# Two-layer transformer block on one core: expert layer by indirect transfers to expert slots and back, in place of all experts on all tokens

## The chip, the cores and the metric

The kernel runs on one core of a Trainium2 chip. The core has five engines that work through their own instruction streams and meet only at semaphores: TensorE (PE; its weight loads are shown apart as PEld), VectorE (DVE), ScalarE (ACT), GpSimd (POOL) and SyncE (SP), which here only starts transfers. All engines but SP compute; TensorE writes into eight banks of PSUM, each 128 partitions by 512 floats. The metric is the device time of one execution in microseconds (us), and lower is better.

## What is computed

Four sequences of 1024 tokens with 128 features go through two layers. The second and third lines below are what the change is about: a router gives each token one of 8 experts, and each expert takes at most 512 tokens (positions are counted in token order, and the comparison is `pos < C`, with positions from 1); a token beyond that gets nothing from the expert layer.

```python
x = x + attention(layernorm(x))              # 16 heads, ALiBi, causal, (4, 1024, 128)
x = x + expert_layer(layernorm(x))           # 8 experts, 4096 tokens, C = 512
x = x + batch_attention(layernorm(x))        # for each position 0..1023: a 4x4 mixing of the sequences
x = x + dense(layernorm(x))                  # one 128x128 product

# expert_layer, x is (4096, 128)
probs = softmax(x @ Wr + br)
gate, idx = max(probs), argmax(probs)
mask = one_hot(idx, E)
pos = cumsum(mask, axis=0) * mask            # place of the token in its expert
mask = mask * (pos < C)
expert_in = gate * mask * x                  # sent to (expert, place)
h = relu(expert_in @ W1[e] + b1[e])
out = gate * mask * (h @ W2[e] + b2[e])      # taken back from (expert, place)
```

The batch attention mixes only the four sequences at one position, so a TensorE tile that holds all four sequences of 32 positions can do it with a mask (`samet`).

## The kernel before, in words

The program has two blocks, with a meeting of all engines between them. The first block is attention. A planner (`plan()`) writes out one order of scores, maxima, exponentials and weighted sums for TensorE, and the other engines follow it. SP's stream in that block carries the operands, the rows of maxima (`q_operand<-max_rows_sb`), the weighted sums to and from DRAM and, late, the residual rows `x_res`. The change touches there the residual loads (`load_residuals`), the bias added to them on GpSimd (`add_bias`) and the transfers placed in SP's stream.

The second block is `later_stages`. Its work comes in 8 chunks of 4 tiles of 128 tokens. Every tile holds 32 positions of all four sequences, so that one layout serves from the attention's output to the last store.

- First stage: for each chunk the sums are divided (`divide`, `reciprocals`), projected (`project`), added to the residual (`add`) and normalised. GpSimd raises to the power -0.5 in three groups, SPANS; ScalarE and VectorE share `apply`. Transposes (`turned`) and logits follow.
- Routing: once for all 32 tiles, on VectorE with three TensorE products for the counts (L1094 to L1128), down to one `gate` for each token, which is 0 for a dropped one.
- Expert loop: 64 slots, one for each pair of chunk and expert. In a slot TensorE multiplies all 512 tokens of a chunk by one expert's W1 (`expert_in`, L1273), adds a large negative number in the columns of tokens of other experts (L1274, `big` by `noth`), ScalarE applies relu with the bias (L1390), and TensorE adds the product with W2 into one bank (`expert_out`, L1282). After 8 experts the bias b2 comes by L1286 and `moe_out` adds the result times the gate. So each token goes through all 8 experts, and 7 of them give zero.
- Batch attention and the dense layer: their steps (t3, u, s, mask, mix, t4, f) are placed by the table SLOTS between the expert slots of the next chunk. Within one chunk they are a chain over four engines; only the steps of the last chunk have no expert slots beside them.

## Time and profile before

| what | us |
|---|---|
| median of 3 runs (798.9 to 801.77) | 799.12 |
| the profiled execution, whole | 797.04 |
| its span from the first to the last instruction | 795.3 |
| TensorE busy in the span | 662.6 |
| VectorE busy | 515.1 |
| ScalarE busy | 448.7 |
| GpSimd busy | 153.8 |
| mean granted clock of TensorE | 0.921 of full |

The profile gives, for each stretch or group of instructions, the time in which an engine was busy, and what ended an idle time before an instruction. TensorE's clock has two levels, 1.2 and 2.4 GHz; a granted clock of 0.50 is the lower and 1.00 the upper. A duration is quoted with the clock where that matters: four transposes take longer at 0.50 than at 1.00. Names such as `ring`, `bank` and `sums` are the PSUM tensors.

### The profile page before, as it was taken

To read this page: it belongs to the slowest core of one execution; us is meant where nothing else is said; L and a number is where in the kernel's file an instruction comes from. 1 tells how busy PE (TensorE), PEld (TensorE's weight loads), DVE (VectorE), ACT (ScalarE), POOL (GpSimd) and SP (SyncE) were. 2 spreads that over 40 slices of the span, in tenths; PEclk is the share of its full clock that TensorE was granted. 3 is DMA by queue.
4 is the path that set the end of the run, shared out by engine and by line. 5 is a ranking of instruction groups with operands and counts; after the bars stand their busy time and mean duration, and the time that the engine had idled before them with its cause. 6 is when DMAs were issued, how large, how long until landed. Compare 5 with 4: busy or idle time off the path is not lost.

```text
span 795.3 us, 14721 instructions
## 1 busy us (share of the span) xinstructions
PE 662.6 (83%) x5478; PEld 315.9 (40%) x5478; DVE 515.1 (65%) x1024; ACT 448.7 (56%) x765; POOL 153.8 (19%) x245
## 2 busy tenths in 40 slices
PE   3656988999989899889899885765799999999953
PEld 2431333333323233333333220455356666666643
DVE  5999788998888888889788830574221345333443
ACT  2950777788777887778777884032234443344310
POOL 2660122212221222212451221030000011010110
PEclk9995899999999999999999998685699999999965
DMA  6494645422212341332203000100000000000001
GB/s 157 133 200 122 160 109 139 107 46 49 52 34 48 72 76 36 75 72 50 50 7 77 6 10 10 28 1 0 1 0 1 10 6 14 14 14 6 9 13 27
DMA packets 49806, 40.58 MB, mean 51 GB/s; under 512 B 9772, under 2 KB 44724, under 8 KB 49724
## 3 DMA queue, kind: packets, MB, share of 16 engines
q1 hardware_dynamic: 43576, 37.22, 20.2%
q10 hardware_dynamic: 6160, 2.43, 1.3%
q8 instruction: 44, 0.72, 0.4%
q14 instruction: 26, 0.21, 0.1%
HBM read 22.32 MB, written 17.04 MB: 49 GB/s over the span
## 4 chain that ended last, share of the span: by engine, by line
PE 62%; DVE 19%; ACT 6%; issue 6%; POOL 3%; DMA 2%; SPq 0%; POOLq 0%; DVEq 0%; ACTq 0%
PE sums L756 15%; DVE neg_max L783 10%; PE ring L735 10%; PE ring L1282 9%; PE ring L1273 8%; PE bank L707 5%; ACT probs L804 5%; PE ring L1274 3%; PE bank L701 2%; DVE probs L506 2%; PE ring L1286 1%; PE bank L1319 1%; PE bank L1222 1%; PE bank L1330 1%; PE ring L718 1%
## 5 line engine op out<-in xcount | busy, mean ns | idle before, releaser
L783 DVE TENSOR_REDUCE neg_max<-bank 128x2 f32<-128x1024 f32 (+2 forms) x320 | 342.8, 1115 | 60.9 <-PE bank L707 58.8
L804 ACT ACTIVATE probs<-ring 128x512 f32<-128x512 f32 (+4 forms) x481 | 301.8, 681 | 79.8 <-PE ring L735 66.8
L735 PE MATMUL ring<-q_operand,k_operand 56*128 56x512 bf16 (+3 forms) x768 | 164.3, 333 | 18.2 <-ACT probs L804 14.5
L756 PE MATMUL sums<-probs,v_all 128*9 128x512 f32 (+3 forms) x1536 | 162.4, 495 | 2.7 <-POOL probs L837 2.1
L707 PE MATMUL bank<-k_operand,q_operand 54*128 54x512 bf16 (+3 forms) x768 | 144.5, 338 | 7.0 <-DVE v_all L514 5.3
L837 POOL TENSOR_SCALAR_AFFINE_SELECT probs<-probs 128x512 f32<-128x512 f32 x128 | 80.2, 635 | 215.6 <-ACT probs L804 214.7
L735 PEld LDWEIGHTS ring<-q_operand,k_operand 56*128 56x128 bf16 x768 | 50.2, 94 | 152.6 <-ACT probs L804 110.5
L1390 ACT ACTIVATE hid<-ring,b1c 128x512 f32<-128x512 f32 x64 | 44.0, 687 | 81.9 <-PE ring L1274 81.7
L701 PE MATMUL bank<-masks 64*128 64x128 bf16 (+2 forms) x768 | 71.9, 224 | 5.2 <-DVE neg_max L783 4.9
L1282 PE MATMUL ring<-w,hid 128*128 128x128 f32 x512 | 74.9, 290 | 0.0
L1273 PE MATMUL ring<-xgt,w 128*128 128x512 f32 x128 | 69.0, 621 | 1.2 <-ACT noth L1382 1.2
L1282 PEld LDWEIGHTS ring<-w,hid 128*128 128x128 f32 x512 | 62.8, 193 | 14.5 <-issue 12.9
L991 POOL TENSOR_TENSOR rs<-ve,half_pow 128x4 f32<-128x4 f32 x16 | 16.1, 1007 | 233.1 <-DVE ve L1011 233.1
L707 PEld LDWEIGHTS bank<-k_operand,q_operand 54*128 54x128 bf16 x768 | 46.1, 97 | 24.5 <-DVE neg_max L783 14.8
L701 PEld LDWEIGHTS bank<-masks 64*128 64x128 bf16 x768 | 36.7, 95 | 37.9 <-DVE neg_max L783 25.4
L1143 DVE SCALAR_TENSOR_TENSOR x_res<-ring,gate,x_res 128x128 f32<-128x128 f32 x32 | 9.0, 344 | 58.8 <-PE ring L1286 58.8
L756 PEld LDWEIGHTS sums<-probs,v_all 128*9 128x9 f32 x1536 | 23.2, 88 | 53.5 <-issue 39.8
L1179 DVE TENSOR_TENSOR res<-x_res,bank 128x512 f32<-128x512 f32 x8 | 5.5, 688 | 54.2 <-PE bank L1330 54.2
L718 PE MATMUL ring<-identb,max_parts 128*32 128x128 bf16 x32 | 7.1, 221 | 24.7 <-POOL max_parts L854 23.5
L1274 PEld LDWEIGHTS ring<-noth,big 8*128 8x128 bf16 x64 | 5.8, 91 | 50.0 <-issue 50.0
L1024 DVE RECIPROCAL denominators<-denominators 128x128 f32<-128x128 f32 x1 | 1.0, 952 | 37.3 <-DMA denominators<-weighted_sums 37.3
L1274 PE MATMUL ring<-noth,big 8*128 8x512 bf16 x64 | 25.1, 392 | 0.0
(156 smaller groups left out, 654.8 us busy)
## 6 DMA issues: line engine op xcount, KB each, us to landing
q_operand<-q_rows SPq DMA_DIRECT2D x64, 96.0 KB, 3.4
k_operand<-k_rows SPq DMA_DIRECT2D x32, 192.0 KB, 4.0
q_rows<-qk_parts SPq DMA_DIRECT2D x36, 128.0 KB, 2.4
k_rows<-qk_parts SPq DMA_DIRECT2D x36, 128.0 KB, 2.4
weighted_sums<-osum SPq DMA_DIRECT2D x128, 18.0 KB
sums_in<-in_L_attn_x SPq DMA_DIRECT2D x4, 512.0 KB, 7.3
q_operand<-max_rows_sb SPq DMA_DIRECT2D x128, 2.0 KB
sums_in<-weighted_sums SPq DMA_DIRECT2D x4, 512.0 KB
```

The lines of the kernel that those rows point to most:

```text
L701: nc.tensor.matmul(ends, masks[rows, 0, a, :], masks[rows, 1, a:a + 1, 64 * a:P].to_broadcast([64, len(pairs), P - 64 * a]), start=a == 0, ...
L707: last = nc.tensor.matmul(ps[:, h, w * j:w * j + w], q_op[rows, buf, t // CH, p, P * (t % CH):P * (t % CH) + P], k_op[rows, buf, p, CW * k ...
L735: last = nc.tensor.matmul(psS[:, bank, w * j:w * j + w], k_op[rows, buf, p, P * kb:P * kb + P], q_op[rows, buf, c, p, q0:q0 + w], start=Tr ...
L756: last = nc.tensor.matmul(psO[32 * i:32 * i + HD + 1, q0:q0 + w], v_all[:, n, kb, i, :], probs[:, u % NPROBS, i // 2, i % 2, 0:w], start=u ...
L783: nc.vector.tensor_reduce(neg_max[:, n % 2, slot, kc, :, pairs[0]:pairs[-1] + 1, t % CH], src, AX.X, ALU.max, negate=True).then_inc(a_read, 1)
L804: nc.scalar.activation(dst, src, ACT.Exp).then_inc(ring_read, 1)
L837: nc.gpsimd.affine_select(out=tri, in_=tri, compare_op=ALU.is_ge, fill=0.0, base=0, pattern=[[0, GH], [1, P]], channel_multiplier=-1).then ...
L991: nc.gpsimd.tensor_tensor(rs[:, :], ve[:, :], half_pow[:, 0:CH], ALU.pow).then_inc(pw_ready, 1)
L1273: nc.tensor.matmul(psZ[n % 2], w1[:, e, :], xgt[:, j % 2, :], start=True, stop=False)
L1274: nc.tensor.matmul(psZ[n % 2], big[:, e, :], noth[:, j % 2, :], start=False, stop=True).then_inc(z_psum, 1)
L1282: nc.tensor.matmul(psY[:, P * i:P * i + P], hid[:, n % 3, P * i:P * i + P], w2[:, e, :], start=(e == 0 and i == 0), stop=False, skip_group ...
L1390: nc.scalar.activation(hid[:, n % 3, :], psZ[n % 2], ACT.Relu, bias=b1c[:, e:e + 1]).then_inc(hid_ready, 1)
```

## The change

It does the expert layer by moving tokens. (1) The residual is held in token order in `rows`, 258 numbers a token: the gated normalised row (XG), the row before the expert layer (X1), the token's number (TOK) and its gate. (2) The first stage of `later_stages` runs in sequence order, tick by tick, with power, scales and `apply` for each chunk, all `apply` on ScalarE. (3) Places are computed in three rounds (tiles 0-15, 16-23, 24-31), by products with a triangle and with ones; place and expert give a row number, `slot`. (4) GpSimd starts 32 indirect transfers, one for each tile, that write each token's 1032 bytes to its row of `expert_rows` in DRAM; dropped tokens have a row number out of bounds. `expert_rows` is cleared by 16 transfers placed in SP's stream during attention. (5) SP waits for all 32, loads each expert's 512 rows, and the experts run once each, on their own rows. (6) GpSimd starts 32 indirect transfers that write each finished row (512 bytes) to its token's row of `x2_rows`; SP waits for all of them. (7) SP loads `x2_rows` in the old layout (32 positions of four sequences), and batch attention and the dense layer run as a loop of 9 ticks, with mask on GpSimd and the scaling of both norms on ScalarE.

The three loops at the end of the diff are VectorE's first stage, TensorE's experts and TensorE's last loop.

```diff
+            def clear_slots(sp, i):
+                n = 2 * P
+                sp.dma_start(slots_dram[n * i:n * i + n, :].rearrange("(p a) f -> p (a f)", a=2),
+                             fill[:, :, :].rearrange("p a f -> p (a f)").bitcast(F32)).then_inc(slots_clear, 16)
...
+                    elif kind == "A" and n >= 5 and args[0] % 8 == 4 and clears:
+                        clear_slots(sp, clears.popleft())
...
-        for j in range(CHUNKS):
-            sp.wait_ge(res_ready, j + 1)
...
+        for k in range(CHUNKS):
+            sp.wait_ge(x1_ready, k + 1)
+            sp.dma_start(x2_dram[CW * k:CW * k + CW, :].rearrange("(u p) d -> p u d", p=P),
+                         rows[:, CH * k:CH * k + CH, X1:X1 + D]).then_inc(x1_out, 16)
+        sp.wait_ge(scattered, 16 * TILES)
+        sp.wait_ge(x1_out, 16 * CHUNKS)
+        for e in range(E):
+            sp.dma_start(es[:, e, :, :].rearrange("p a f -> p (a f)"),
+                         slots_dram[CAP * e:CAP * e + CAP, :].rearrange("(p a) f -> p (a f)", a=CH)).then_inc(es_in[e], 16)
+        sp.wait_ge(x2_out, 16 * E * CH)
+        for j in range(CHUNKS):
+            for b in range(B):
+                src = x2_dram[S * b:S * b + S, :].rearrange("(u t) d -> t u d", t=32)
+                sp.dma_start(x2[32 * b:32 * b + 32, CH * j:CH * j + CH, :], src[:, CH * j:CH * j + CH, :]).then_inc(x2_in[j], 16)
...
+        def send_rows(u):
+            pool.wait_ge(row_ready, u + 1)
+            nc.gpsimd.indirect_dma_start(
+                out=slots_dram, out_offset=bass.IndirectOffsetOnAxis(ap=slot[:, u:u + 1], axis=0), in_=rows[:, u, :],
+                in_offset=None, bounds_check=E * CAP - 1, oob_is_err=False).then_inc(scattered, 16)
+        def send_tokens(e, a):
+            pool.wait_ge(ye_ready, e + 1)
+            nc.gpsimd.indirect_dma_start(
+                out=x2_dram, out_offset=bass.IndirectOffsetOnAxis(ap=es[:, e, a, TOK:TOK + 1].bitcast(U32), axis=0),
+                in_=ye[:, e, a, :], in_offset=None, bounds_check=B * S - 1, oob_is_err=False).then_inc(x2_out, 16)
...
+        for t in range(TICKS):
+            if t < CHUNKS:
+                add(t)
+                if t + 1 < CHUNKS:
+                    divide(t + 1)
+                scales(t)
...
+        for e in range(E + 1):
+            if e + 1 < E:
+                columns_of(e + 1)
+            if e < E:
+                expert_in(e)
+            if e >= 1:
+                expert_out(e - 1)
...
+        for t in range(CHUNKS + 1):
+            if t >= 1:
+                mixed(t - 1)
+            if t < CHUNKS:
+                t3(t)
+                u_of(t)
+            if t >= 1:
+                t4(t - 1)
+            if t < CHUNKS:
+                scores(t)
+            if t >= 1:
+                f(t - 1)
```

On GpSimd, in the second block, stand before only the powers of the norms.

```order
L988 TENSOR_TENSOR rs<-ve,half_pow 128x16
L988 TENSOR_TENSOR rs<-ve,half_pow 128x8 x2
L991 TENSOR_TENSOR rs<-ve,half_pow 128x4 x16
L261 UNCONDITIONAL_BRANCH
```

And now, at the same place of GpSimd's stream:

```order
L998 TENSOR_TENSOR rs<-ve,half_pow 128x4 x8
L1002 DMA expert_rows<-rows,slot 4096x258 x32
L1008 DMA x_rows<-ye,rows 4096x128 x32
L1014 TENSOR_TENSOR rs<-ve,half_pow 128x4
L1018 TENSOR_TENSOR ee<-ee,samet 128x512
L1014 TENSOR_TENSOR rs<-ve,half_pow 128x4 x2
L1018 TENSOR_TENSOR ee<-ee,samet 128x512
```

All 64 indirect transfers stand in one row between the powers of the first stage and those of the last, and the mask `ee<-ee,samet` has come from VectorE to GpSimd.

On TensorE, late in the second block of the kernel before, the steps of batch attention stand singly between expert products (a step of one chunk: L1305 is u, L1309 the scores, L1325 the transposes t4).

```order
L1305 MATMUL bank_0<-xt,aqk 128x512
L1273 MATMUL ring<-xgt,w 128x512
L1274 MATMUL ring<-noth,big 128x512
L1282 MATMUL ring<-w,hid 128x128 x4
L1309 MATMUL bank_0<-ut,xt 128x128 x4
L1325 MATMUL bank_1<-ident,xn 128x128 x4
L1273 MATMUL ring<-xgt,w 128x512
L1274 MATMUL ring<-noth,big 128x512
L1282 MATMUL ring<-w,hid 128x128 x4
L1330 MATMUL bank_1<-wft,xt 128x128 x4
```

And now, one tick of the last loop on TensorE, from one t3 (L1326) to the next:

```order
L1326 MATMUL bank_0<-ident,xe 128x128 x4
L1333 MATMUL bank_0<-xt,aqk 128x512
L1357 MATMUL ring<-ident,xn 128x128 x4
L1340 MATMUL bank_1<-ut,xt 128x128 x4
L1365 MATMUL ring<-wft,xt 128x128 x4
L1349 MATMUL bank_1<-xe,ee 128x129 x2
L1349 MATMUL ring<-xe,ee 128x129 x2
L1326 MATMUL bank_0<-ident,xe 128x128 x4
```

No product stands between the steps that is not itself a step of the chunk or of the chunk before; t4 of the chunk before stands ahead of the scores of this one.

On SP, after attention, stood only the stores; now three more kinds of transfer stand ahead of them.

```order
L972 DMA x_rows<-rows 128x4x128 x8
L977 DMA rows<-expert_rows 128x1032 x8
L983 DMA xn<-x_rows 32x4x128 x32
L988 DMA out<-res 32x4x128 x32
```

The expert loads stand behind a wait for all 32 transfers to the slots, the loads of `x2_rows` behind one for all 32 transfers back.

## Rows read from the trace of the kernel before

**Rows 1.** Busy time by stretches of the second block (us, instruction counts, granted clock, DMA)

```profile
502.60:548.65 46.05, 36.63 (x176) 29.67 (x176) 26.90 (x113) 10.96 (x24) 6.40 (x3) 0.72 0.00 1
548.65:560.60 11.95, 0.82 (x3) 0.28 (x3) 10.92 (x37) 0.42 (x1) 0.00 (x0) 0.50 0.00 0
560.60:759.20 198.60, 196.56 (x1050) 123.00 (x1050) 68.56 (x312) 75.46 (x122) 13.09 (x13) 0.97 0.03 8
759.20:795.30 36.10, 15.31 (x55) 11.63 (x54) 15.50 (x68) 3.46 (x6) 3.02 (x3) 0.54 0.08 20
```

**Rows 2.** In order of time: batch attention of the last chunk, no expert work beside it

```profile
765.38 2.09 PE L1319 MATMUL bank<-xe,ee 128*128 128x129 f32 x8 [6.17 <-DVE ee L1157]
767.26 1.06 PE L1301 MATMUL bank<-ident,xe 128*128 128x128 f32 x4
767.77 1.13 DVE L1168 SCALAR_TENSOR_TENSOR x_res<-bank,inv,x_res 128x128 f32<-128x128 f32 x4
768.35 0.59 ACT L1401 COPY xt<-bank 128x512 f32<-128x512 f32 x1 [12.36 <-PE bank L1301]
768.99 2.08 PE L1305 MATMUL bank<-xt,aqk 128*128 128x512 f32 x2 [0.68 <-ACT xt L1401]
774.48 0.63 ACT L1412 ACTIVATE ee<-th 128x512 f32<-128x512 f32 x1
775.64 2.07 PE L1330 MATMUL bank<-wft,xt 128*128 128x128 f32 x8 [0.97 <-ACT xt L1417]
...
790.93 0.69 DVE L1179 TENSOR_TENSOR res<-x_res,bank 128x512 f32<-128x512 f32 x1 [3.96 <-PE bank L1330]
```

**Rows 3.** Busy time by short stretches, the granted clock (columns as in rows 1)

```profile
525.00:530.00 5.00, 5.00 (x20) 3.97 (x19) 3.19 (x17) 2.69 (x6) 1.64 (x1) 0.50 0.00 0
530.00:535.00 5.00, 2.83 (x25) 2.73 (x24) 4.01 (x23) 2.16 (x6) 0.81 (x1) 0.99 0.02 5
...
770.00:775.00 5.00, 4.00 (x14) 2.53 (x12) 1.99 (x12) 1.70 (x3) 1.01 (x1) 0.50 0.00 0
```

**Rows 4.** In order of time (start, duration): where the second block begins

```profile
502.63 0.95 DVE L1024 RECIPROCAL denominators<-denominators 128x128 f32<-128x128 f32 x1 [37.29 <-DMA denominators<-weighted_sums]
...
509.17 0.69 DVE L1039 TENSOR_TENSOR x_res<-x_res,ring 128x512 f32<-128x512 f32 x1 [1.02 <-PE ring L1203]
```

**Rows 5.** In order of time: pieces of a norm, and a scaling on ScalarE

```profile
522.32 1.65 ACT L1353 ACTIVATE xn<-x_res,nt,rs 128x128 f32<-128x128 f32 x4 [29.58 <-DVE nt L1060]
...
760.40 0.87 DVE L1006 BATCH_NORM_STATS2 stats<-x_res 128x6 f32<-128x128 f32 x4
761.31 0.38 DVE L1009 BATCH_NORM_AGGREGATE mv<-stats 128x2 f32<-128x6 f32 x4
761.73 0.17 DVE L1011 TENSOR_SCALAR ve<-mv 128x4 f32<-128x4 f32 x1
761.98 1.01 POOL L991 TENSOR_TENSOR rs<-ve,half_pow 128x4 f32<-128x4 f32 x1 [13.28 <-DVE ve L1011]
```

**Rows 6.** GpSimd by shape: busy us, mean ns of one, idle before

```profile
L862 POOL TENSOR_TENSOR x_res<-x_res,bob 128x512 f32<-128x512 f32 x8 | 10.2, 1271 | 0.0
...
L988 POOL TENSOR_TENSOR rs<-ve,half_pow 128x16 f32<-128x16 f32 x1 | 2.9, 2914 | 27.2 <-DVE ve L1051 27.2
```

**Rows 7.** SP's issues of one transfer to DRAM (duration ns: min/median/max)

```profile
L671 SPq DMA_DIRECT2D weighted_sums<-osum x8: 264/315/317, 485.0 to 493.8; - x8
```

**Rows 8.** Transfers by line: count, KB each, us from issue to landing

```profile
x_res<-in_L_attn_x SPq DMA_DIRECT2D x4, 512.0 KB, 5.3
out<-res SPq DMA_DIRECT2D x32, 64.0 KB, 1.8
```

**Rows 9.** GB/s moved, in 40 equal slices of the span

```profile
GB/s 157 133 200 122 160 109 139 107 46 49 52 34 48 72 76 36 75 72 50 50 7 77 6 10 10 28 1 0 1 0 1 10 6 14 14 14 6 9 13 27
```

**Rows 10.** In order of time: products of the same shapes at the upper clock

```profile
653.76 1.06 PE L1309 MATMUL bank<-ut,xt 128*128 128x128 f32 x8
654.66 0.60 PE L1325 MATMUL bank<-ident,xn 128*128 128x128 f32 x4
```

879 lines of the change are left out of this document (432 added, 447 removed).

## The prediction, made before the changed kernel was run

> **What bounds the kernel now.** I read first the busy time by stretches. After attention, which ends at 502.6 us, the second block has four stretches [rows 1]: 46.1 us to the logits, 12.0 of routing with TensorE all but idle, 198.6 in which TensorE is busy for 196.6 (expert products for all tokens, with the steps of batch attention and the dense layer between them), and 36.1 in which the last chunk's chain runs out. So TensorE's work bounds the long stretch, and most of that work is multiplied by zero. Next come the rows of the last chunk, where the chain over the engines lies open: each step starts 0.03 to 0.05 us after the one before it ends, and the products take twice as long as earlier, since the granted clock is 0.50 [rows 2, 3]. That open chain is what I need, because the new last loop consists of it.
>
> **First stage (new), until the first row can be sent.** It starts as before: the reciprocal ends the wait at 502.6, the first add begins at 509.2 [rows 4]. A tick on VectorE is the add 0.69, statistics 0.87 and 0.38, variance 0.17, GpSimd's power 1.01 (the division, 0.69, lies under it) and four short operations of 0.2: 3.9, with the passages between engines 4.2 [rows 2, 5]. TensorE's tick is two sets of eight pieces (up to 2.07 each), one of transposes (1.06) and the logits (at most 2.07, eight pieces with fewer columns): 7 at the lower clock, half at the upper [rows 2, 10]. The clock moved between both levels in this stage before [rows 3]; I take 5.0 a tick, between the ends 4.2 and 7. Seven ticks bring the eighth add to 544.2. Ahead of the first places TensorE still has the transposes and logits of two chunks (3.0), then 16 products with ones; an fp32 piece costs 0.26 (2.07 for eight) [rows 2], these are bf16 and mostly shorter, I take 0.13, 2.1 in all. Placing is eight short operations (2.0), gating one tile 0.4 on ScalarE (1.65 for four) [rows 5]. The first row can go at **551.5**. Two more rounds of some 10 us make the last rows ready near 571.
>
> **Sending, 32 indirect transfers.** They stand in one row on GpSimd, and everything later waits for all of them. No row shows an indirect transfer. Below, SP starts a small plain one in 0.32 [rows 7], but SP makes no list of 128 addresses. Above, GpSimd's dearest operation here is 2.91 [rows 6]. I take **1.3**, near GpSimd's pass over 128 x 512 elements, 1.27 [rows 6], as the kind of work that this engine does in software over 128 partitions; 0.32 and 2.91 stay for the range. 32 x 1.3 = 41.6 brings the last issue to 593.1; the rows, ready by 571, are not the bound. Landing takes 2.0 (1.8 for a store of 64 KB [rows 8]): 595.1.
>
> **Experts.** SP loads 528 KB an expert. The first lands 5.3 later, as 512 KB do [rows 8]; the next follow by 2.6 each if the fastest slice so far, 200 GB/s, holds [rows 9]. On TensorE the transposes of the third expert stand ahead of the first W2 product, so the first result waits for the third load, 10.6 after issue; then 1.06 + 2.08 + 2.07 on TensorE, 0.69 and 1.13 on VectorE [rows 2], 0.3 of passages: 17.9, so 613.0. From there GpSimd's other 32 issues bound: an expert costs TensorE 5.2 at the lower clock and 2.7 at the upper, four issues 5.2. 41.6 lead to 654.6, landing, four loads' issue and the landing of these (2.0 + 1.8 + 1.8 [rows 8]) to **660.2**. What the change removes is the whole of the 198.6: 64 expert slots become 8. What takes their place up to here is 102 us (551.5 to 653, of which 83 are issues).
>
> **The last loop.** Before, these steps cost only their TensorE time, since expert products filled the gaps. Now there is nothing to fill them, and a tick is a ring. From the end of one chunk's scores: tanh 0.6, exponential 0.63, the copy 0.59 for the dense product of the chunk before and that product 2.07 (it stands ahead of the mixing on TensorE; GpSimd's mask, 1.27 [rows 6], is ready sooner), mixing 2.09; on VectorE reciprocals 0.25, weighting 1.13, moments 1.59 and the scales of the next chunk 0.8, which stand behind them; ScalarE's scaling 1.65; transposes 1.06, copy 0.59, u 2.08, copy 0.59, ScalarE's second scaling 1.65, its transposes 1.06, the next scores 2.07 [rows 2, 5]. Sum 20.5, with 15 passages of 0.05 **21.2 us**. TensorE is busy for 10.4 of them. At 4.00 of 5 us busy in short pieces the clock stayed at 0.50 [rows 3], so I take the lower level. The first chunk's scores and exponential come 13.2 after the load (moments, power, scales, scaling, the same products), seven periods are 148.4, the way out from the last exponential 16.2: 660.2 + 177.8 = 838.0, and the last store adds 3.7, as now (790.93 + 0.69 to 795.3 [rows 1, 2]).
>
> **Attention.** SP gets 16 more transfers of 264 KB, each in front of rows of maxima for which TensorE waits later. At 200 GB/s one holds up the next by 1.3, so the bounds are 0 and 21; a gain is excluded, as nothing is taken from this stream. The rows of maxima have slack and the transfers are spread over eight groups of heads; I take 0.
>
> **Sum.** 841.7 for the span against 795.3. The profiled execution took 797.04, 1.7 more than its span, and the median of the runs is 2.1 above that: 843.4 and **845.5**; I forecast 845.
>
> **Weighed against the Trainium skill.** The traces show a store of 64 KB landing after 1.8 [rows 8], while SP starts the next after 0.32 [rows 7], so transfers overlap. The Trainium skill (DMA: Bandwidth & Descriptors, Anatomy of one DMA) gives about 2.0 us fixed for a transfer from GpSimd plus its bytes at 436 GB/s. Were 64 of them to run one after another, that would be an estimated 142 in place of 83, and the time 905; no row here shows whether they overlap.
>
> **Rivals.** (a) Issues as cheap as SP's, 0.32. Then the rows' readiness bounds the sending (571 in place of 593, -22) and TensorE and the loads bound the experts (seven periods of about 3, -19): 804. For it: transfers overlap on SP. Against: GpSimd takes 1.01 even for 128 x 4 powers [rows 5]. (b) The faster side: TensorE's clock rises in the last loop and stays. Then four products of a tick lose 1.01 each and two sets of transposes 0.46 [rows 2, 10], the period is 16.2, and the loop with its ends is 40 shorter: 805; the kernel is faster than 799 if besides an issue costs less than 1.2, and with 1.0 it takes 786. For it: dense product and mixing follow one another without a gap for 4.2 us, and 5.0 busy of 5 were followed by 0.99 [rows 3]. Against: 5.6 us of idling follow each time. (c) Transfers of GpSimd do not overlap; each holds the next until it lands. By the 1.8 of a store [rows 8] that is 64 x 1.8 = 115 for 83: 877. (d) An issue costs what GpSimd's dearest operation does, 2.91: 64 x 1.6 more, 948.
>
> **Chances.** Forecast with issues of 1.0 to 1.75: 0.64 (826 to 874 by 64 x the price). (a) 0.09, (b) 0.10, (c) 0.10, (d) 0.07. The range leaves out (b) and (d): **800 to 885**, with the cost in attention and the first stage's clock (4.2 to 7 a tick, -6 to +14) in it. Half a per cent is about what a measurement of this kernel can tell from no change. Faster by more: 0.10; within: 0.05 (a good part of (a), since 804 is near the bound); slower: 0.85.
>
> **What would show it.** In the changed kernel's trace: mean length of GpSimd's stretch with 32 issues (1.3 each; 0.3 and 2.9 are the rivals'); VectorE and TensorE idle through both of them; a period of 21 between the stores of the chunks, with granted clock 0.50 (16 and 1.00 for (b)); attention ending within 2 us of 502.6. It would be wrong if the price of an issue is off by 0.5 (32 us), if the chunk ring overlaps more than I see, or if the cleared rows hold up attention.

## The result: 3% slower, and where the time went

The changed kernel took 822.57 us in the median of four runs, 820.86 the fastest, beside 799.01 for the kernel before in the same comparison. The fourth run, 836.65, had a lower granted clock (0.733 in place of 0.81 to 0.82) and does not enter the ratio. The ratio is 1.031, with a 95% interval of 1.027 to 1.035. The forecast was 845 in a range of 800 to 885. The direction and the range held; the time came 22 us below the forecast. The profiled execution took 823.1, with a span of 821.1 against 795.3 before.

I read the busy time by stretches first, as for the kernel before. This is the view of the changed kernel, with the stretches cut at the events that the sum used; the columns are those of [rows 1]: the stretch, its length, busy time (and instructions) of PE, PEld, DVE, ACT and POOL, granted clock, DMA share, GB/s.

```profile
0.00:504.10 504.10, 416.42 (x4195) 152.18 (x4195) 393.76 (x497) 358.63 (x612) 130.83 (x227) 0.94 0.36 86
504.10:550.60 46.50, 32.17 (x218) 29.35 (x218) 32.14 (x146) 17.46 (x44) 8.07 (x8) 0.79 0.15 46
550.60:591.50 40.90, 8.20 (x80) 7.55 (x79) 9.06 (x48) 7.11 (x24) 31.40 (x32) 0.50 0.16 55
591.50:606.20 14.70, 9.80 (x43) 6.91 (x44) 2.32 (x6) 4.46 (x8) 0.01 (x1) 0.64 0.75 289
606.20:647.00 40.80, 11.02 (x70) 8.42 (x68) 12.19 (x35) 5.73 (x9) 31.33 (x32) 0.66 0.09 27
647.00:651.60 4.60, 0.00 (x0) 0.00 (x0) 0.00 (x0) 0.00 (x0) 0.03 (x1) 0.50 0.28 81
651.60:664.80 13.20, 5.26 (x14) 3.00 (x14) 3.64 (x24) 4.04 (x8) 1.05 (x1) 0.50 0.46 134
664.80:801.70 136.90, 64.89 (x230) 47.17 (x230) 41.12 (x234) 41.98 (x91) 22.69 (x21) 0.59 0.05 12
801.70:821.10 19.40, 6.99 (x28) 6.00 (x28) 4.80 (x22) 2.66 (x6) 2.28 (x2) 0.50 0.12 27
```

Rows 1 had 198.6 us in which TensorE was busy for 196.6. That stretch is gone. In its place stand two stretches of 41 us in which GpSimd issues without pause and the others mostly wait (third and fifth line), 15 us between them in which loads and the first experts run, and a last loop of 137 us in which TensorE is busy for 65. The change took away 45% of TensorE's busy time in the second block (138.3 us of products where there were 249.3, and most of what is left runs at the lower clock) and put more waiting than that in its place: from its first operation the block takes 317.4 us (503.7 to 821.1) where it took 292.7 (502.6 to 795.3).

**The sends.** The groups of the page for GpSimd (line, engine, operation, names, count, then busy us and mean ns, then idle time before):

```profile
L1008 POOL DMA_INDIRECT x_rows<-ye,rows x32 | 31.4, 980 | 24.2 <-DVE ye L1155 15.3
...
L1002 POOL DMA_INDIRECT expert_rows<-rows,slot x32 | 31.4, 982 | 13.7 <-issue 7.9
```

An indirect transfer of 128 rows keeps GpSimd for 0.98 us, whether its rows are long (`expert_rows`, the first stage) or short (`x_rows`). Between two of them lie 0.30 us in which the engine waits for nothing that is shown. The pitch is 1.28, and 32 of them are the 41 us.

**The last loop.** One tick of the changed kernel at the lower clock, in order of time (start, duration, engine, line, operation, names, and the idle time before with its releaser), some operations left out:

```profile
703.47 0.57 ACT L1475 COPY xt<-ring 128x512 f32<-128x512 f32 x1
703.64 1.27 POOL L1018 TENSOR_TENSOR ee<-ee,samet 128x512 f32<-128x512 f32 x1 [11.61 <-ACT ee L1470]
704.09 2.07 PE L1365 MATMUL ring<-wft,xt 128*128 128x128 f32 x8 [1.82 <-ACT xt L1475]
...
706.81 1.07 PE L1349 MATMUL ring<-xe,ee 128*128 128x129 f32 x4
707.92 0.17 DVE L1183 RECIPROCAL inv<-bank 128x2 f32<-128x2 f32 x1 [12.95 <-PE ring L1349]
...
708.19 0.61 DVE L1188 SCALAR_TENSOR_TENSOR xn<-bank,inv,xn 128x128 f32<-128x128 f32 x2
...
709.35 0.87 DVE L1163 BATCH_NORM_STATS2 stats<-xn 128x6 f32<-128x128 f32 x4
...
711.63 1.65 ACT L1446 ACTIVATE xe<-xn,nt 128x128 f32<-128x128 f32 x4 [7.59 <-DVE nt L1177]
...
713.33 1.12 PE L1326 MATMUL bank<-ident,xe 128*128 128x128 f32 x4 [5.45 <-ACT xe L1446]
...
715.12 2.07 PE L1333 MATMUL bank<-xt,aqk 128*128 128x512 f32 x2 [0.68 <-ACT xt L1456]
717.23 0.58 ACT L1458 COPY ut<-bank 128x512 f32<-128x512 f32 x1 [2.16 <-PE bank L1333]
717.71 1.65 ACT L1446 ACTIVATE xn<-xn,nt 128x128 f32<-128x128 f32 x4
719.41 1.12 PE L1357 MATMUL ring<-ident,xn 128*128 128x128 f32 x4 [2.22 <-ACT xn L1446]
...
720.32 1.91 PE L1340 MATMUL bank<-ut,xt 128*128 128x128 f32 x8
722.27 0.60 ACT L1465 ACTIVATE th<-bank 128x512 f32<-128x512 f32 x1 [2.91 <-PE bank L1340]
722.90 0.63 ACT L1470 ACTIVATE ee<-th 128x512 f32<-128x512 f32 x1
```

This is the open chain of [rows 2], but of every chunk: nearly always one engine at a time. Where the chain passes from one engine to another, the next step begins 0.03 to 0.06 us after the end of the one before. Between the mixing and the next chunk's transposes stands VectorE: it weights the mixed rows (L1188), takes their moments (from L1163 on), and only then makes the scales of the next chunk (L1174 to L1177), which need nothing of this one. VectorE waits 12.95 us for the mixing, GpSimd 11.61 for the exponential, once in every tick. The distances between the eight masks are 19.1, 19.7, 20.0, 20.0, 18.2, 20.0 and 20.0 us, 19.6 on average.

The granted clock of 0.59 says less than it seems to. This is the same tick in three parts (columns as above):

```profile
704.05:708.00 3.95, 3.79 (x16) 3.50 (x16) 0.08 (x1) 0.00 (x0) 1.83 (x2) 0.50 0.00 0
708.00:711.00 3.00, 0.00 (x0) 0.00 (x0) 2.84 (x17) 0.00 (x0) 0.01 (x1) 1.00 0.00 0
711.00:723.60 12.60, 6.01 (x18) 3.75 (x18) 3.25 (x18) 5.66 (x13) 1.00 (x1) 0.52 0.09 21
```

After the dense product and the mixing (3.79 us of TensorE) the upper level was granted, for 3 us in which TensorE had nothing to do, and it was gone again before the next product.

### The profile page after: what moved, and what is told of

Same layout as the page of the kernel before. It is cut to its first block, busy times and chain, and to the rows that moved or that the text cites. A ratio compares the mean times of both kernels' runs of the same rounds, so it can differ in the third digit from the quotient of the medians.

```text
span 821.1 us, 13686 instructions
## 1 busy us (share of the span) xinstructions
PE 554.7 (68%) x4875; PEld 260.6 (32%) x4875; DVE 499.0 (61%) x1010; ACT 442.1 (54%) x799; POOL 227.7 (28%) x323
## 4 chain that ended last, share of the span: by engine, by line
PE 46%; DVE 19%; ACT 12%; issue 9%; POOL 8%; DMA 3%; SPq 1%; POOLq 0%; DVEq 0%; ACTq 0%
PE sums L772 15%; PE ring L751 10%; DVE neg_max L799 9%; PE bank L723 5%; ACT probs L820 5%; POOL x_rows L1008 3%; POOL expert_rows L1002 2%; PE bank L1333 2%; PE bank L717 2%; PE bank L1340 2%; PE ring L1365 2%; ACT xn L1446 2%; DVE probs L517 1%; ACT xe L1446 1%; PE bank L1326 1%
## 5 line engine op out<-in xcount | busy, mean ns | idle before, releaser
L1446 ACT ACTIVATE xe<-xn,nt 128x128 f32<-128x128 f32 x32 | 13.2, 482 | 89.9 <-DVE nt L1177 89.9
L1326 PE MATMUL bank<-ident,xe 128*128 128x128 f32 x32 | 8.9, 435 | 77.8 <-ACT xe L1446 77.8
L1008 POOL DMA_INDIRECT x_rows<-ye,rows x32 | 31.4, 980 | 24.2 <-DVE ye L1155 15.3
L1018 POOL TENSOR_TENSOR ee<-ee,samet 128x512 f32<-128x512 f32 x8 | 10.2, 1270 | 91.8 <-ACT ee L1470 91.8
L1002 POOL DMA_INDIRECT expert_rows<-rows,slot x32 | 31.4, 982 | 13.7 <-issue 7.9
L1163 DVE BATCH_NORM_STATS2 stats<-xn 128x6 f32<-128x128 f32 x64 | 14.0, 281 | 34.7 <-DMA xn<-x_rows 31.7
L1386 ACT ACTIVATE xn<-rows,nt,rs 128x128 f32<-128x128 f32 x32 | 13.2, 482 | 38.9 <-DVE nt L1080 38.9
L1326 PEld LDWEIGHTS bank<-ident,xe 128*128 128x128 f32 x32 | 5.7, 217 | 79.8 <-ACT xe L1446 79.8
L1151 DVE TENSOR_TENSOR yb<-ring,b2b 128x512 f32<-128x512 f32 x8 | 5.5, 690 | 38.6 <-PE ring L1307 38.6
L1293 PE MATMUL bank<-ident,rows 128*128 128x128 f32 x32 | 6.3, 332 | 33.4 <-DMA rows<-expert_rows 33.3
```

Of the source, the lines that this page charges most:

```text
L1002: nc.gpsimd.indirect_dma_start(out=slots_dram, out_offset=bass.IndirectOffsetOnAxis(ap=slot[:, u:u + 1], axis=0), in_=rows[:, u, :], in_of ...
L1008: nc.gpsimd.indirect_dma_start(out=x2_dram, out_offset=bass.IndirectOffsetOnAxis(ap=es[:, e, a, TOK:TOK + 1].bitcast(U32), axis=0), in_=ye ...
L1326: last = nc.tensor.transpose(psT3[:, P * i:P * i + P], xe[:, j % 2, i, 0:D], ident[:, :])
L1446: last = nc.scalar.activation(dst, x2[:, CH * j + i, :], ACT.Identity, bias=nt[:, z, 1, i:i + 1], scale=nt[:, z, 0, i:i + 1])
```

## The experiments

Twelve runs were made in three groups of four. The kernels of one group ran on the same chip beside the kernel before (median 797.0, 798.7 and 794.3 us in the three). Times are medians, ratios are to the kernel before of the same group. `after_again` is the changed kernel itself and `f_late_b` is `f_late` once more; all others but `best`, `best2` and `best2_fill` differ from the changed kernel in one thing (`early` in two that go together). Eight of the twelve, the first and the third group, hold stalls of up to some 12 us that are the subject of part C, so their whole times are not to be set beside those of the second group.

### A. The last loop: clock, order, overlap

**filled**: does the granted clock set a quarter of a tick?

```diff
+        def busy(n):
+            for i in range(n):
+                nc.tensor.matmul(banks[7][:, 0:P], ident[:, :], aqk[:, :], start=True, stop=True)
         for t in range(CHUNKS + 1):
             if t >= 1:
                 mixed(t - 1)
+                busy(10)
             if t < CHUNKS:
                 t3(t)
+                busy(1)
                 u_of(t)
+                busy(4)
...
                 scores(t)
+                busy(3)
```

> The changed kernel with 18 products of 128x128 on constants into an unused bank put into TensorE's idle stretches of every tick of the last loop (10 ahead of the mixing, 1 ahead of u, 4 behind it, 3 behind the scores); nothing reads them. At the lower clock they take about 0.52 us each and fit the gaps of 5.4, 0.7, 2.2 and 1.8 us that the trace of the changed kernel shows. Theory A, the granted clock sets a quarter of each tick: the chain of one tick holds 9.9 us of products at the lower clock, which are 5.3 at the upper one, so if the fillers bring the clock up, the seven periods fall from 19.6 to about 15.5 us, the way out by 2, and the time from 822.6 to about 790 (ratio to the kernel before 0.99). Theory B, the products are not what a tick waits for (it is the other engines' chain): with the clock up the periods stay near 19 and the time near 820. If the clock stays at 0.50 the run shows only that fillers cost nothing: 822 to 826.

The ten stand behind the mixing, ahead of the next transposes, and not ahead of the mixing as the expectation says. It took 813.87 us, ratio 1.020 (1.014 to 1.025), with some 11 us of the stalls of part C. Two ticks of it by stretches (columns as above):

```profile
711.08:727.58 16.50, 10.81 (x70) 8.95 (x70) 6.16 (x35) 6.06 (x14) 3.25 (x3) 0.90 0.07 17
760.14:777.15 17.01, 11.88 (x70) 9.87 (x70) 6.17 (x35) 6.06 (x14) 3.24 (x4) 0.80 0.07 15
```

The clock is 0.8 to 0.9 in place of 0.59, and a tick takes 16.7 us on average where the changed kernel has 19.6. That is 2.9 less, not the 4.1 of theory A and far from theory B's 0.6. Most of the missing part is in one product. u stands behind the transposes and ScalarE's copy, and it still runs at the lower clock, for the whole or a part, in each of the seven ticks, as here:

```profile
713.42 2.40 PE L1370 MATMUL sums<-aqk,ident 128*128 128x128 f32 x20
...
720.36 2.08 PE L1333 MATMUL bank<-xt,aqk 128*128 128x512 f32 x2 [0.39 <-ACT xt L1464]
...
725.15 1.06 PE L1340 MATMUL bank<-ut,xt 128*128 128x128 f32 x8
```

The fillers (x20 are ten products) end near 715.8, TensorE stands idle until 719.0, and u, a little later, takes 2.08; the scores, which stand behind four fillers and the second transposes, take 1.06. So the mechanism of rival (b) is real: the clock costs about 3 us a tick of the average 19.6, and 3.5 of a tick that is all at the lower level. But the kernel as it is doesn't get it back, and fillers that leave one gap don't get all of it.

**f_late**: the dense product of a chunk behind the next mixing instead of ahead of it.

```diff
             if t >= 1:
                 mixed(t - 1)
+            if t >= 2:
+                f(t - 2)
...
                 scores(t)
-            if t >= 1:
-                f(t - 1)
+        f(CHUNKS - 1)
```

> The changed kernel with one order changed: on TensorE the dense product f of a chunk stands behind the next chunk's mixing instead of ahead of it. Theory A, a tick is one chain through TensorE's queue and f (2.07 us from the copy's end) stands in it ahead of the mixing by 1.2 us (the mask ended 704.91, the mixing began about 706.1): each of seven periods loses 1.2 us, 822.6 becomes about 814 (ratio to the kernel before 1.02). Theory B, another chain of the same length runs through f, its addition and the buffers that they free: no change, 822. The last chunk's f is where it was, so the way out doesn't change.

It took 827.85 us, ratio 1.038 (1.033 to 1.043): 5 us more than the changed kernel in its own comparison. The loop itself did get shorter, as its masks show:

```profile
675.15 1.27 POOL L1018 TENSOR_TENSOR ee<-ee,samet 128x512 f32<-128x512 f32 x1 [10.51 <-ACT ee L1471]
...
807.23 1.26 POOL L1018 TENSOR_TENSOR ee<-ee,samet 128x512 f32<-128x512 f32 x1 [11.61 <-ACT ee L1471]
```

The seven periods are 132.1 us against 136.9: theory A, though smaller. In the six profiles with the unchanged loop they are 133.7 to 137.3, by how many ticks had the upper level for the mixing, so the gain is to be read from ticks of one kind. A tick at the lower clock is 19.13 in place of 19.97 (0.84, where I had written 1.2), and the ticks in which the mixing falls into the upper clock are 18.2 in both kernels: there f takes 1.16, and the mixing begins 0.18 after the mask's end with it and 0.05 without. The 5 us are lost elsewhere: the first mask comes at 675.15 and not at 664.82. That is the subject of part C.

**pipelined**: the next chunk made independent of this one's mixing.

```diff
+        for t in range(2):                     # VectorE
+            moments_in(t)
+            normal_scales(0, t)
         for t in range(CHUNKS + 2):
+            if t >= 2:
+                add_out(t - 2)
+            if t < CHUNKS:
+                mix(t)
+                if t + 2 < CHUNKS:
+                    moments_in(t + 2)
+                normal_scales(1, t)
+                if t + 2 < CHUNKS:
+                    normal_scales(0, t + 2)
...
+            mask(t)                            # GpSimd
+            power_of(1, t)
+            if t + 2 < CHUNKS:
+                power_of(0, t + 2)
...
+                mixed(t)                       # TensorE
+                t3(t + 1)
+                u_of(t + 1)
+                scores(t + 1)
+                f(t - 1)
+                t4(t)
```

ScalarE follows in the same order: scaling of t+1, copy of t-1, copies of t+1, second scaling of t, tanh and exponential of t+1.

> The changed kernel with the last loop alone rewritten: the same instructions, but moments, power and scales of chunk t+2 are made in tick t, so that the normalization, scores and exponentials of chunk t+1 need nothing of chunk t's mixing, and f and its copy are one tick later. Theory A, the 19.6 us of a tick come from the order, in which VectorE makes the next chunk's scales only behind the mixing's sums: with the two chains side by side a tick falls to what the longer chain and TensorE's 9.3 us of products at the lower clock allow, about 12 us; seven periods save 53 us and the time is about 769 (ratio to the kernel before 0.96). If the denser TensorE also gets the upper clock, about 755. Theory B, the time of a tick is bound by buffers that two chunks share and by queues (ScalarE's 6 us, VectorE's 6 us): 16 us a tick, about 797.

It took 771.47 us, ratio 0.966 (0.961 to 0.971), with 11.4 us from mask to mask on average. Theory A held (about 12 a tick and 769 were expected), although some 12 us of stalls (part C) are in this time, so that 769 was met in part by luck. The same instructions in another order make the seven periods 57 us shorter, 79.5 in place of 136.9, so the 19.6 were no engine's bound. The clock is not what did it: in best, which has the same loop, ticks with a granted clock of 0.50 to 0.53 take 11.5 us as well.

### B. The sends

**half_sends**: are the issues the path?

```diff
         for e in range(E):
-            for a in range(CH):
+            for a in range(CH // 2):
                 send_tokens(e, a)
...
-        sp.wait_ge(x2_out, 16 * E * CH)
+        sp.wait_ge(x2_out, 16 * E * CH // 2)
```

> The changed kernel with 16 of the 32 transfers that send the experts' results back (two of four for each expert); half of the results are left out, so the time is only a price. Theory A, the stage is one queue of issues on GpSimd at 1.28 us each and all of it lies on the path: 16 x 1.28 = 20.5 us less, 802 us, the level of the kernel before. Theory B, the experts' work or the landings set the end of the stage: 5 us less or nothing, 817 to 822.

It leaves out half of the results, so its time is only a price. It took 810.1 us, ratio 1.019 (1.012 to 1.026). In the same group f_late_b, which has all 32, took 829.2. From the first to the last of these issues there are now 21.9 us (611.83 to 633.72), where f_late_b has 45.6 (611.00 to 656.63). 16 issues at 1.28 are 20.5, and 19 are seen in the whole time, although f_late_b's loop is the faster by some 5. What is left of the 23.7 between 21.9 and 45.6 goes with the stalls of part C, of which half_sends has fewer in this stage. Theory B's 5 us are excluded: the issues lie on the path.

**half_rows**: is the price one of rows?

```diff
-                ...ap=es[:, e, a, TOK:TOK + 1].bitcast(U32), axis=0),
-                in_=ye[:, e, a, :],
+                ...ap=es[0:64, e, a, TOK:TOK + 1].bitcast(U32), axis=0),
+                in_=ye[0:64, e, a, :],
```

> The changed kernel with each of the 32 transfers that send the experts' results back cut from 128 rows to 64; half of the results are left out, so the time is only a price. Theory A, GpSimd's 0.97 us for one such transfer is work for each row: it falls to about 0.6 us and the second stage of sends takes 29 us instead of 41, 12 us less in all. Theory B, it is a fixed price of one instruction: 0.97 us stays, the stage takes 40.8 us and the time stays within 1 us of the changed kernel on this chip.

It too leaves out half of the results. It took 818.75 us, ratio 1.026 (1.022 to 1.031), 4 us below the unedited kernel of its group (822.8); its five runs lie between 815.2 and 823.3, and the stage of these sends is 2.1 us shorter (37.8 from first to last issue in place of 39.9). The group of these issues, from the lines of half_rows:

```profile
L1008 POOL DMA_INDIRECT x_rows<-ye,rows x32 | 29.2, 913 | 23.8 <-DVE ye L1155 15.2 <-issue 8.5
```

Half of the rows take 0.91 us in place of 0.98. Nearly all of the price belongs to the instruction (theory B), and about 0.001 us, an estimate from this difference, to a row. Fewer transfers would help; smaller ones don't.

**early**: begin the sends a round sooner.

```diff
-    ROUNDS = [(0, 16), (16, 24), (24, 32)]
-    ROUND_AT = [CHUNKS - 2, CHUNKS, CHUNKS + 2]
+    ROUNDS = [(0, 8), (8, 16), (16, 24), (24, 32)]
+    ROUND_AT = [CHUNKS - 4, CHUNKS - 2, CHUNKS, CHUNKS + 2]
...
         for k in range(CHUNKS):
             power(k)
+            if k == CHUNKS - 2:
...
+                for u in range(3):
+                    send_rows(u)
```

> The changed kernel with four rounds of choosing (8 tokens' tiles each) in place of three (16, 8, 8), so that the first 8 tiles have their slots a round earlier, and three of the 32 sends issued between the last two of the first stage's powers on GpSimd. Theory A, the sends are one queue of 32 x 1.28 us which begins when the first round is placed: it begins 10 to 11 us earlier, less about 3 us that one more round costs VectorE; 7 to 9 us less than the changed kernel on the same chip. Theory B, the end of the sends is set by the last round (its tiles are placed last) or by the stores behind: no gain, up to 3 us lost by the added round.

It took 814.04 us, ratio 1.020 (1.015 to 1.026), 8.8 less than the unedited kernel of the group. The first send is at 544.0 in place of 553.3, the first mask at 660.5 in place of 666.7. Of the gain 6.2 us stand before that mask; the loop, which is the same, happened to be 1.8 shorter in this profile. Theory A: a queue that bounds is worth starting early, even at the price of one more round on VectorE.

**clears_late**: the 16 clears behind attention instead of in it.

```diff
-                    elif kind == "A" and n >= 5 and args[0] % 8 == 4 and clears:
-                        clear_slots(sp, clears.popleft())
...
                 load_sums(sp, B - 1)
+                while clears:
+                    clear_slots(sp, clears.popleft())
```

> The changed kernel with the 16 clears of the slots issued behind attention, ahead of the first stage's stores, instead of inside attention. Theory A, the clears cost attention the 1.1 us by which it ends later than in the kernel before (503.69 against 502.63): it ends near 502.6, and since the sends begin 46 us later the clears' 16 issues at 0.32 us are hidden: 821.5 (within 0.3% of the changed kernel). Theory B, the 1.1 us is spread of the executions: attention ends anywhere between 502 and 504.5, the time is the same. Theory C, the clears now collide with the first stage's stores and loads and the sends wait for them: up to 10 us longer, 832.

It took 836.8 us, ratio 1.047 (1.042 to 1.053), the worst of all. Theory C, but at another place than it said. SyncE's queue and VectorE's first operation of the second block, in order of time:

```profile
500.57 0.59 SPq L328 DMA_DIRECT2D denominators<-weighted_sums  x1
501.21 10.80 SPq L440 DMA_DIRECT2D expert_rows<-fill  x16
...
512.46 0.95 DVE L1049 RECIPROCAL denominators<-denominators 128x128 f32<-128x128 f32 x1 [43.39 <-PEq L371]
```

In f_late, of the same group, the reciprocal starts at 502.64 and the first addition at 509.13. Here they start at 512.46 and 517.94. SyncE needs 10.80 us for the 16 issues, 0.68 each where a single one takes 0.32 [rows 7]. Meanwhile the clears' 4.2 MB move at 327 GB/s from 504 to 508 and 361 from 508 to 512; that the issues waited for this traffic is likely but not shown. Its last issue ends at 512.01, and TensorE and VectorE both begin the second block at 512.46, released by the instruction that ends the first block (L371), which waits for SyncE too. So 16 issues that I had called hidden lie on the path, because SyncE's queue ends a block that the other engines wait for. As to attention's end, the reciprocal started at 503.69 and 504.64 in the two profiles of the changed kernel, at 502.64 and 505.10 in f_late and filled, which have the same attention. In all twelve profiles with the clears inside attention it starts between 501.8 and 507.3, 503.8 on average, and there is one profile of the kernel before. So theory B: the 1.1 us can't be told from the spread. clears_late itself says the same. Its attention has no clears, yet SyncE's load of the denominators, which follows attention's last results, is issued at 500.57, where the others have 495.5 to 500.7.

### C. Stalls in half of the runs

**after_again**: the changed kernel, unedited.

> The changed kernel once more, unedited, beside the next three. In the first four experiments VectorE and ScalarE stood still five to seven times for 5 to 15 us each while GpSimd issued its transfers, in the rows as waits for 'remote', 24 to 27 us of it on VectorE before the last send of results, and the two stages of sends ended 10 to 13 us later than in the profile of the changed kernel, which has no such wait. Theory A, the stalls belong to the chip or the hour and not to the edits: this run shows them too and takes 830 to 835 us (ratio 1.04), and the 5 us by which the late f was slower turn into a gain of 5 to 8 against this run. Theory B, they belong to the edited kernels' code: this run has none and takes 822.

It took 822.82 us, ratio 1.031 (1.027 to 1.036), and had none of the stalls. Nor had early, best and half_rows, its neighbours. That the unedited kernel had none spoke for theory B, that three edited ones had none spoke against it, so one of the stalling kernels was run again.

**f_late_b**: f_late, unedited.

> The same kernel as f_late, once more on whatever chip this call gets. There it took 827.9 with five waits for 'remote' of 5 to 15 us; the unedited changed kernel, run later, had none and took 822.8. Theory A, the stalls belonged to the chip or the hour of the first four experiments: none here, and since the mask-to-mask periods of f_late were 18.9 us on average against 19.4, the time is about 818 (ratio 1.025). Theory B, the stalls belong to the code of this kernel: they are here again and it takes 828 (ratio 1.038).

It took 829.22 us, ratio 1.042 (1.036 to 1.049), with the stalls, and so had its three neighbours, half_sends among them, which differs from half_rows and from the changed kernel in nothing ahead of the second stage of sends. What a stall looks like in f_late, GpSimd in order of time:

```profile
579.15 0.97 POOL L1002 DMA_INDIRECT expert_rows<-rows,slot  x1 [0.30 <-issue]
586.72 1.05 POOL L1002 DMA_INDIRECT expert_rows<-rows,slot  x1 [6.59 <-DVE rows L1145]
```

and its waits from 500 us on, by engine and line (us in all, times, longest):

```profile
DVE yb L1151 <- remote: 20.2, 2, 15.1
DVE pos L1113 <- remote: 13.7, 2, 7.6
...
ACT xgt L1424 <- remote: 8.7, 1, 8.7
```

VectorE and ScalarE stand still at five lines in all (the other two are L1087 and L1430), at three to five of the same operations in each of these profiles, in the two stages in which GpSimd sends. The products that they wait for had ended before: L1087 goes on at 575.25, and its logits on TensorE were done at 558.2. In f_late the first stage of sends is 6 us longer for it (46.2 from first to last issue in place of 39.9) and the second 5 (44.6 in place of 39.8). All eight profiles of the first and third group have the stalls; the four of the second group and the first profile of the changed kernel have none. Groups divide them, and half_sends has them in the first stage of sends, ahead of its edit, where half_rows has none. That speaks against the edits. It does not point to one chip either: by its number the second and third group had the same chip (11), the first another (5). And no kernel was in both camps. So the cause stays open. It follows that a difference between groups counts only within a stage, and that f_late's "5 us slower" is not in its loop, which is shorter; whether its code has a part in the stalls, the runs can't tell.

### D. A version that beats both

**best**: pipelined and early together.

> Both edits in one: the last loop with two chunks side by side (771.5 against 797.0 of the kernel before, ratio 0.966) and the earlier rounds and sends. Theory A, the two gains lie in different stages, one behind the other, and add: 762 to 765 us, ratio 0.956 to 0.96. Theory B, what is sent earlier waits at the end of the sends: 771.

It took 756.98 us, ratio 0.949 (0.944 to 0.955): 41.7 less than the kernel before and 65.8 less than the changed one. The gains add, as in theory A; it is faster than the 762 to 765 expected, which were reckoned from pipelined's 771.5 with its stalls. By stretches:

```profile
503.70:542.40 38.70, 27.22 (x182) 25.45 (x183) 28.33 (x127) 14.27 (x37) 7.07 (x7) 0.81 0.16 48
...
659.40:736.80 77.40, 50.21 (x230) 36.65 (x230) 40.22 (x230) 41.16 (x91) 21.99 (x21) 0.74 0.09 20
```

The last loop (the last line) has shrunk from 136.9 to 77.4. Counted from the reciprocal, the first send comes after 38.7 us where after_again has 48.7, and since the last of the first stage's 32 then comes 42.9 us later instead of 39.9, 7 of these 10 us are kept. So the idea of the change was good for 5%, and the order of the steps in the last loop had eaten it.

**best2** and **best2_fill**: the second normalization one tick later again, then fillers ahead of the loop and in it.

```diff
                 t3(t + 1)                      # TensorE, best2
                 u_of(t + 1)
+                t4(t - 1)
                 scores(t + 1)
                 f(t - 1)
-                t4(t)
...
+        busy(150)                              # best2_fill, ahead of the loop
...
+            busy(2)                            # ahead of mixed(t) and of u_of(t + 1)
```

On ScalarE the second scaling, now that of chunk t-1, moves behind the first one of chunk t+1.

> The fastest so far (best, 757.0) with the second normalization of a chunk one tick later again: on ScalarE tanh and exponential no longer stand behind it, and its transposes stand on TensorE between u and the scores. Theory A: in best a tick takes 11.5 us where the clock was 0.50 (TensorE's chain) and 10.56 where it was 0.96 (there tanh waited 2.7 us behind the normalization in ScalarE's queue). At the upper clock a tick falls to 8.5, at the lower it stays 11.5 to 11.9: with three or four of seven ticks at the upper clock 6 us less, about 751; if the clock stays at the lower in all ticks, 760. Theory B, VectorE's 6.7 us with its waits for GpSimd's powers set the tick: 10.3, no change, 757.

> The kernel best2 with products on constants that nothing reads: 150 of 128x128 (0.24 us each at the upper clock by the experiment filled) in the 39 us in which TensorE stands idle while results are sent, and 2 ahead of each mixing and 2 ahead of each u. Theory A, it is the idle stretch ahead that lets the last loop begin at 0.50: it begins at the upper clock, keeps it, and all ticks take 8.5 to 9: 20 us less than best2 at the lower clock, about 738 in all. Theory B, the level follows what TensorE does in the ticks themselves and the stretch ahead is forgotten within a tick or two: the same ticks as best2, plus 4 fillers of 0.24 to 0.5 us: 0 to 8 us more.

They took 758.26 us (0.954, 0.946 to 0.961) and 762.72 us (0.959, 0.953 to 0.965), both with the stalls of their group. Within the loop best2 has 10.0 us from mask to mask where best has 11.0, and best2_fill has 9.3, so the edit gains some 7 us in the loop that the stalls hide. Its fastest ticks take 8.0 us, where theory A had 8.5. Whether best2 is faster than best as a whole was not measured: the two were never in one group, and one has the stalls and the other not. The masks of best2_fill:

```profile
677.91 1.26 POOL L1018 TENSOR_TENSOR ee<-ee,samet 128x512 f32<-128x512 f32 x1 [13.35 <-ACT ee L1485]
685.93 1.26 POOL L1018 TENSOR_TENSOR ee<-ee,samet 128x512 f32<-128x512 f32 x1
697.47 1.26 POOL L1018 TENSOR_TENSOR ee<-ee,samet 128x512 f32<-128x512 f32 x1 [2.24 <-ACT ee L1485]
705.50 1.26 POOL L1018 TENSOR_TENSOR ee<-ee,samet 128x512 f32<-128x512 f32 x1
```

The ticks are 8.0, 11.5, 8.0, 10.7 us and so on by turns. By stretches, the granted clock in 680 to 690 and in 690 to 700:

```profile
680.00:690.00 10.00, 5.62 (x36) 4.22 (x35) 7.90 (x40) 4.56 (x10) 3.24 (x3) 0.94 0.00 0
690.00:700.00 10.00, 8.61 (x44) 6.76 (x43) 4.81 (x30) 6.49 (x16) 3.28 (x3) 0.72 0.09 20
```

The loop began at the upper clock, as meant, and already in the second tick it was gone for a part: theory B. In 680 to 690 TensorE is busy for 5.62 of 10 us, in 690 to 700 for 8.61, and the tick that follows is a fast one again. The filling ahead was also sized wrongly. The stall of the experts pushed it back, it ended at 672 and held up the first chunk's transposes, whose input was ready at 661.8. The first mask comes 8.5 us later than in best2, more than the 4.7 that the loop gains.

## Why the prediction was right, and where its sizes were off

The steps, each against the profile of the changed kernel:

| step | predicted us | measured us |
|---|---|---|
| attention's end, first operation of the block | 502.6 | 503.7 |
| to the first send | 551.5 | 550.6 |
| 32 issues | 41.6 (1.3 each) | 40.9 (1.28 each) |
| landing, until SP starts the experts' loads | 2.0 | 1.2 |
| to the experts' first result | 17.9 | 13.5 |
| 32 issues | 41.6 | 40.8 |
| landing, four loads | 5.6 | 4.6 |
| first chunk to its exponential | 13.2 | 13.2 |
| seven periods | 148.4 (21.2 each) | 136.9 (19.6 each) |
| way out and last store | 19.9 | 19.4 |
| span | 841.7 | 821.1 |

**Right: the price of an issue.** It was a guess between 0.32 and 2.91, put at 1.3 for its nearness to GpSimd's pass over 128 x 512 elements [rows 6]. The sum of work and gap is 1.28. That closeness is luck in part, as half_rows showed: the price is not the pass over rows that I had likened it to, but a fixed one. Rivals (a) and (d) are excluded. So is (c), by the transfers of the changed kernel (issuing engine, count, median us to landing):

```profile
expert_rows<-rows,slot POOLq DMA_INDIRECT x32, 2.3
x_rows<-ye,rows POOLq DMA_INDIRECT x32, 2.2
```

In the median each lands 2.2 to 2.3 us after its issue, while the next is issued after 1.28: two are under way at once. The Trainium skill (DMA: Bandwidth & Descriptors, Anatomy of one DMA) gives about 2.0 us fixed for a transfer from GpSimd, and the trace's 2.2 agrees; read as a price for each one in turn it would have given 905, and the overlap takes it out of the sum.

**Off: the term of the last loop, by 11.5 us.** I laid all pieces and 15 passages end to end for 21.2. At the lower clock the tick measures 19.97. The order of time above shows most of the 1.2 in small overlaps at the queues: the dense product and the mixing, 4.16 in the sum, take 3.8 from f's start to the reciprocal; the second transposes and the scores, 3.13 in the sum, take 2.8, since pieces of two products overlap on TensorE; the second scaling, and the copy for the dense product, start 0.1 before what stands ahead of them on ScalarE ends. These are 0.8; the rest is spread over the passages and VectorE's short operations. The other 0.4 of the average are ticks in which the upper clock was granted for a part, as in the second of these two ticks of the changed kernel, where the dense product and the mixing ran at the upper level and all others at the lower (in the first, all at the lower):

```profile
703.64:723.61 19.97, 9.80 (x34) 7.24 (x34) 6.17 (x35) 6.06 (x14) 3.25 (x4) 0.59 0.06 14
743.57:761.80 18.23, 8.06 (x34) 5.60 (x34) 6.17 (x35) 6.06 (x14) 3.24 (x3) 0.65 0.06 14
```

Rival (b) was judged rightly: the clock averaged 0.59 in the loop, so it did not rise and stay, and filled showed that its mechanism would have been worth 3 us a tick. But it did rise, in each of the ticks looked at above, and was spent on an idle TensorE; the prediction's reason for the lower level, 4.00 of 5 us busy without a rise, says nothing of that.

**Off: the experts' first result, by 4.4 us.** Two terms were too long and one was missing. The third set of transposes, which I had at 10.6 us after the first load's issue, began after 7.4 (592.72 to 600.13). From there to the end of the first product with W2 it took 3.4 in place of 5.2, since TensorE's clock rose meanwhile: 0.50 from 596.2 to 600.4, 0.66 to 603.0 and 1.00 to 606.2. And GpSimd's first issue came 0.8 after VectorE's last operation, so that the part behind that product took 0.6 more than the sum has. As to the loads, I let them run at 200 GB/s, the fastest slice of the kernel before [rows 9]. That kernel never asked for more, and a rate that nobody demanded was no bound. GB/s of the changed kernel in 40 slices of 540 to 670 us, with the three slices of the experts' loads:

```profile
GB/s 0 81 0 41 86 125 90 90 59 46 36 29 38 25 23 11 128 399 418 358 25 45 29 9 60 23 10 40 43 9 2 16 29 70 137 139 136 137 41 0
```

At 400 GB/s an expert's 528 KB take an estimated 1.3 us and not 2.6. The Trainium skill (DMA: Bandwidth & Descriptors, Anatomy of one DMA) has 436 GB/s as the rate in its formula, which is one for transfers from GpSimd; the 418 of a slice, in loads from SP, come near it.

**Off by little:** the first stage (47.0 us from the reciprocal to the first send, in place of 48.9). The clock was 0.79, and six of its seven ticks took 4.3 us on average in place of my 5.0; the seventh took 7.1, because the first part of the routing stands on VectorE ahead of the last addition, which I had not seen. Also off by little: the two landings, 0.8 and 1.0 too long; attention, 1.1 too short, which clears_late and the spread between profiles don't let one tell from nothing. The step from the span to the time was off too: I had added 2.1 us from the profiled execution to the median, and here the median lies 0.5 below it.

**What the prediction did not ask.** It treated the ring of the last loop as given by the data. The experiment pipelined shows that the order of the steps tied one chunk to the next. It changes the order on four engines at once, so how much of the 57 us VectorE's alone is worth was not measured.

## What to carry to other kernels

When a change removes work from the engine that bounds, ask what that work had been covering: here 64 expert slots had hidden a chain of 20 us per chunk, and without them the chain was the time. Price a queue of instructions on one engine by its pitch and start it as early as its first input allows; giving each transfer fewer rows buys almost nothing. And before a ring of steps over four engines is taken as the cost of a loop, look for the place where an in-order engine makes chunk t+1 wait for chunk t, here the next chunk's scales behind this chunk's mixing on VectorE; the new order around it was worth 57 us, more than the change had lost.

## What the runs showed of the hardware

- An indirect transfer issued from GpSimd costs that engine 0.98 us for 128 rows and 0.91 for 64, and 0.30 more before the next, the same for long rows and short ones. It lands 2.2 to 2.3 us after issue in the median, and the next is issued before it lands.
- SP's loads of 516 KB (528,384 bytes) each moved 358 to 418 GB/s in a slice, about twice the 200 of the fastest slice of the kernel before.
- TensorE's granted clock moved between its two levels within a tick; in the changed kernel the upper one was granted for 3 us in which TensorE was idle (708 to 711), and the products around it ran at the lower. In filled a product ran at the lower level after an idle stretch of about 3 us although the stretches average 0.90; in best2_fill fast and slow ticks took turns, 8.0 and 11 us.
- In eight of thirteen profiles VectorE and ScalarE stood still, mostly for 5 to 15 us at a time, while GpSimd sent indirect transfers, at three to five of the same operations each time; the kernels of one group all had it or none did, and two groups with the same chip number differed. Its cause is open.
